# Second attention: the maximum's split in two-input operations, POOL's squaring in one addition and with a larger share

## What is computed

```python
S = jnp.einsum('bhnd,bhmd->bhnm', Q, K) / dh ** 0.5
W_tau = jax.nn.softmax(S, axis=-1)
W_sigma = 1.0 / ((1.0 + jnp.abs(S) / b_) ** 2 + t_ ** 2)
W_sigma = W_sigma / W_sigma.sum(axis=-1, keepdims=True)
tau = jnp.einsum('bhnm,bhmd->bhnd', W_tau, V).transpose(0, 2, 1, 3).reshape(B, N, D)
sigma = jnp.einsum('bhnm,bhmd->bhnd', W_sigma, V).transpose(0, 2, 1, 3).reshape(B, N, D)
f = 0.5 * tau + 0.5 * sigma
```

## Time and profile before

| | |
|---|---|
| time, median of 3 runs | 3559.43 us (3557.44 to 3564.81) |
| profiled execution, span | 3560.9 us |
| DVE busy in it | 2905.9 us, 82% |
| TensorE busy | 2950.8 us, 83% |
| ACT busy | 2449.7 us, 69% |
| POOL busy | 1854.7 us, 52% |
| products on POOL (L1402), 256 | 923.0 us, mean 3606 ns |
| large additions on POOL (L1399), 256 | 453.4 us, mean 1771 ns |
| squares on DVE (L1628), 256 | 222.1 us, mean 867 ns |
| casts on DVE (L1567), 64 | mean 2505 ns |
| narrow additions on POOL (L1397), 256 | 75.9 us, mean 297 ns |

### The profile page before, as it was taken

How to read it: one execution, slowest core, us unless ns; L and a number is a source line. 1 busy time by engine, 2 the same in 40 slices (tenths; PEclk the granted TensorE clock), 3 DMA queues, 4 the chain that set the end, 5 groups by cost and what they waited for, 6 DMA issues and landing times. The chain is left out here.

```text
span 3560.9 us, 64791 instructions
## 1 busy us (share of the span) xinstructions
PE 2950.8 (83%) x19824; PEld 1285.0 (36%) x19824; DVE 2905.9 (82%) x5109; ACT 2449.7 (69%) x3005; POOL 1854.7 (52%) x1283
## 2 busy tenths in 40 slices
PE   4987999999798897478788788878878888885699
PEld 3753444444576454222222222222222222222455
DVE  5996777777499666699999999999999999997665
ACT  3973656656497453288888888888888888885354
POOL 3210000000121444188888888888888888885354
PEclk9987999999799798699999989998999999897699
DMA  3002111110000000200000000000000000000000
GB/s 88 0 0 99 35 33 33 32 33 25 1 1 0 1 1 0 81 14 11 10 13 10 10 11 13 10 10 12 12 10 11 13 10 10 12 5 1 1 13 12
DMA packets 48969, 62.18 MB, mean 17 GB/s; under 512 B 8464, under 2 KB 27920, under 8 KB 48880
## 3 DMA queue, kind: packets, MB, share of 16 engines
q1 hardware_dynamic: 48880, 61.08, 5.5%
HBM read 45.60 MB, written 14.68 MB: 17 GB/s over the span
## 5 line engine op out<-in xcount | busy, mean ns | idle before, releaser
L1402 POOL TENSOR_TENSOR a_sg<-a_sg,a_shifted 128x1600 f32<-128x1600 f32 x256 | 923.0, 3606 | 21.4
L1524 ACT ACTIVATE a_pt<-a_pb 128x1024 f32<-128x1024 f32 x512 | 526.5, 1028 | 310.0 <-PE a_pb L1442 308.8
L1604 DVE TENSOR_REDUCE a_mx<-a_pm 128x1 f32<-128x1024 f32 x512 | 622.5, 1216 | 89.3 <-PE a_pm L1442 81.6
L1612 DVE TENSOR_SCALAR a_sg<-a_pa 128x1024 int32<-128x1024 int32 x512 | 617.3, 1206 | 29.0 <-PE a_pa L1442 28.3
L1287 DVE TENSOR_REDUCE a_mx<-a_pm 128x1 f32<-128x512 f32 (+3 forms) x768 | 404.0, 550 | 158.6 <-PE a_pm L1126 150.4
L1458 PE MATMUL a_po<-a_pt,a_Vh 128*32 128x512 f32 x2048 | 527.8, 639 | 2.2 <-ACT a_sg L1543 2.2
L1458 PE MATMUL a_po<-a_sg,a_Vh 128*32 128x512 f32 x2048 | 527.7, 639 | 0.0
L1214 ACT ACTIVATE a_pt<-a_pb 128x512 f32<-128x512 f32 (+3 forms) x768 | 337.2, 501 | 268.6 <-PE a_pb L1140 96.4
L1539 ACT ACTIVATE a_sg<-a_sg,a_parh 128x2048 f32<-128x2048 f32 x256 | 514.0, 2008 | 0.0
L1543 ACT ACTIVATE a_sg<-a_sg 128x2048 f32<-128x2048 f32 x256 | 492.5, 1924 | 0.0
L1399 POOL TENSOR_SCALAR a_shifted<-a_sg,a_parh 128x1584 f32<-128x1584 f32 x256 | 453.4, 1771 | 0.1
(11 more groups left out here) (244 smaller groups left out, 6061.9 us busy)
## 6 DMA issues: line engine op xcount, KB each, us to landing
all_Q<-q_parts SPq DMA_DIRECT2D x384, 48.0 KB
all_K<-k_parts SPq DMA_DIRECT2D x384, 48.0 KB
q_parts<-p_parts SPq DMA_DIRECT2D x16, 384.0 KB, 2.6
k_parts<-p_parts SPq DMA_DIRECT2D x16, 384.0 KB, 2.6
all_Q<-a_rows SPq DMA_DIRECT2D x128, 6.0 KB
out_dram<-all_X SPq DMA_DIRECT2D x8, 256.0 KB, 2.3
sw_raw<-in_f_We_dram SPq DMA_DIRECT2D x1, 1024.0 KB, 7.1
sw_raw<-in_f_w_gP_dram SPq DMA_DIRECT2D x1, 704.0 KB, 11.0
```

What stands on the lines that cost most here:

```text
L1402: nc.gpsimd.tensor_tensor(buf[:, :, 0:CUT], buf[:, :, 0:CUT], shifted[:], ALU.mult)\
L1524: nc.scalar.activation(pt[(j - LT) % 4][:, i, :], pb[:], ACT.Exp, scale=SC)\
L1604: nc.vector.tensor_reduce(mx[:, (j // PER) % 2, t:t + 1], pm[:], AX.X, ALU.max)\
L1612: nc.vector.tensor_scalar(sg[(j - LS) % 4][:, i, :].bitcast(I32), pa[:].bitcast(I32), SIGN_OFF, None, ALU.bitwise_and).then_inc(abs_done, 1)
```

## The change

For the split, the reduction L1604 now negates what it writes, so mx holds the negated maximum (low). The first part is written as the larger of low and low, a two-input operation that only rounds to bf16. The second part is low minus the first part, rounded; the remainder in fp32 is the same difference, not rounded; the third part is the remainder minus the second part. These are four operations instead of five, each a TENSOR_TENSOR with both inputs in SBUF, and the last, which signals parts_ready, stands behind the second reduction instead of the second sign-clearing.

On POOL the narrow addition is gone: one addition covers all columns below CUT, and CUT rises from 800 to 864 columns, so POOL's addition and product have 1728 elements and DVE's square has 320. The wait for the parameters stands ahead of the wait for the sign-clearings, and that wait is followed by a NOP of its own. The parameters of a head are copied one head earlier. The matmuls are the same.

```diff
--- before.py
+++ after.py
@@ -1313,8 +1313,7 @@
     UNROLL = PER * RING
     LS, LT, LE, LP = 4, 6, 6, 7
     SC = DH ** -0.5
-    EDGE = 8
-    CUT = 25 * T // 32
+    CUT = 27 * T // 32
     with ExitStack() as ctx:
         m = Mem(nc, ctx, tag)
         Q, K = ([stack[:, r, :] for r in range(RING)] for stack in stacks)
@@ -1383,22 +1382,24 @@
                     if (j - LS) % PER == 0:
                         if some(h, 2):
                             pool.wait_ge(pv_done, PER * (h - 1))
-                        nc.gpsimd.tensor_copy(parh[:, ((j - LS) // PER) % RING, :], par[:, h, :])\
-                            .then_inc(par_ready, 1)
+                        if not some(h):
+                            nc.gpsimd.tensor_copy(parh[:, 0, :], par[:, h, :]).then_inc(par_ready, 1)
+                        if not (isinstance(h, int) and h + 1 >= HEADS):
+                            nc.gpsimd.tensor_copy(parh[:, ((j - LS) // PER + 1) % RING, :], par[:, h + 1, :])\
+                                .then_inc(par_ready, 1)
                         nc.gpsimd.tensor_copy(Vh[:, ((j - LS) // PER) % 2, :, 0:DH + 1], V[:, h, :, :])\
                             .then_inc(vh_ready, 1)
                     buf = sg[(j - LS) % 4]
                     if some(s):
                         pool.wait_ge(sq_pool, s)
+                    pool.wait_ge(par_ready, h + 1)
                     pool.wait_ge(abs_done, 2 * s + 2)
-                    pool.wait_ge(par_ready, h + 1)
+                    pool.nop(nofuse=True)
                     b2 = parh[:, ((j - LS) // PER) % RING, 0:1]
 
-                    nc.gpsimd.tensor_tensor(shifted[:, :, 0:EDGE], buf[:, :, 0:EDGE],
-                                            b2.unsqueeze(2).broadcast_to([P, 2, EDGE]), ALU.add).then_inc(shift_done, 1)
-                    nc.gpsimd.tensor_scalar(shifted[:, :, EDGE:CUT], buf[:, :, EDGE:CUT], b2, 1.0, ALU.add, ALU.mult)\
+                    nc.gpsimd.tensor_scalar(shifted[:], buf[:, :, 0:CUT], b2, 1.0, ALU.add, ALU.mult)\
                         .then_inc(shift_done, 1)
-                    pool.wait_ge(shift_done, 2 * s + 2)
+                    pool.wait_ge(shift_done, s + 1)
                     nc.gpsimd.tensor_tensor(buf[:, :, 0:CUT], buf[:, :, 0:CUT], shifted[:], ALU.mult)\
                         .then_inc(sq_pool, 1)
 
@@ -1552,23 +1553,21 @@
 
                     if j % PER or at(it, j, 1) is None:
                         return
-                    h, top = head(it, j, 1), mx[:, ((j - 1) // PER) % 2, :]
+                    h, low = head(it, j, 1), mx[:, ((j - 1) // PER) % 2, :]
                     if n == 0:
                         dve.wait_ge(max_red, TT * h + TT)
                         if some(h):
                             dve.wait_ge(rows_turned, h)
-                        nc.vector.tensor_scalar(neg3[:, 0, :], top, -1.0, None, ALU.mult).then_inc(chain, 1)
-                    else:
-                        dve.wait_ge(chain, 4 * h + n)
+                        nc.vector.tensor_tensor(neg3[:, 0, :], low, low, ALU.max).then_inc(chain, 1)
                     if n == 1:
-                        nc.vector.scalar_tensor_tensor(rem[:], top, -1.0, neg3[:, 0, :], ALU.mult, ALU.subtract)\
-                            .then_inc(chain, 1)
+                        dve.wait_ge(chain, 3 * h + 1)
+                        nc.vector.tensor_tensor(neg3[:, 1, :], low, neg3[:, 0, :], ALU.subtract).then_inc(chain, 1)
                     if n == 2:
-                        nc.vector.tensor_copy(neg3[:, 1, :], rem[:]).then_inc(chain, 1)
+                        nc.vector.tensor_tensor(rem[:], low, neg3[:, 0, :], ALU.subtract).then_inc(chain, 1)
                     if n == 3:
-                        nc.vector.tensor_tensor(rem[:], rem[:], neg3[:, 1, :], ALU.subtract).then_inc(chain, 1)
-                    if n == 4:
-                        nc.vector.tensor_copy(neg3[:, 2, :], rem[:]).then_inc(parts_ready, 1)
+                        dve.wait_ge(chain, 3 * h + 3)
+                        nc.vector.tensor_tensor(neg3[:, 2, :], rem[:], neg3[:, 1, :], ALU.subtract)\
+                            .then_inc(parts_ready, 1)
 
                 def output(it, j, n):
 
@@ -1601,8 +1600,8 @@
                         if sm is not None:
                             t = 2 * (j % PER) + i
                             dve.wait_ge(max_mm, 2 * sm + i + 1)
-                            nc.vector.tensor_reduce(mx[:, (j // PER) % 2, t:t + 1], pm[:], AX.X, ALU.max)\
-                                .then_inc(max_red, 1)
+                            nc.vector.tensor_reduce(mx[:, (j // PER) % 2, t:t + 1], pm[:], AX.X, ALU.max,
+                                                    negate=True).then_inc(max_red, 1)
                         part(it, j, 2 * i + 1)
                         output(it, j, 2 * i)
                         if ss is not None:
```

## The result

The changed kernel takes 3569.52 us (median, 3565.82 to 3571.20) against 3561.15 for the kernel before, run on the same chip: a ratio of 1.0021, 95% interval 1.0014 to 1.0028. It is slower by 0.2%, 8 us; the forecast was slower by 107. The profiled execution has a span of 3565.8 us and a mean granted clock of 0.894 (3560.9 and 0.911 before).

The account below looks back on a forecast made before the run. Bound: a chain through DVE and POOL in the second attention. Per head 10.11 + 5.89 + 2 x 5.93 + 0.92 = 28.78 us, +1.7 on 27.06, times 63 = +107 us: median 3666 us, range 3530 to 3690.

Parts of the forecast that it names:

- (a): POOL's pieces in the second attention: product grows from 3.61 to 3.88 us, large addition from 1.58 to 1.71 us.
- (b): DVE's square, 320 elements instead of 448, takes 0.12 to 0.13 us less: 0.35 after a product, 0.55 alone.
- (c): Slots paced by POOL: late slot 5.93 us for 5.82, slot after the head slot 5.89 for 5.63; +0.48 per head.
- Nearly free: POOL's narrow addition was said to cost almost nothing today, ending about 0.07 us after the square's end.
- (d): Head slot: first split operation held 1.5 us by POOL's addition, second 2.9 by its product; 10.11 us for 8.87, +1.24.
- E: The end of DVE's square L1628, the moment from which the slots of a head are timed.
- slow-clock time: Late slots after TensorE's wait, put to its 1.2 GHz clock: 0.92 us per head, bounds 0 and twice that.
- (e): Parts ready before the last sign-clearing: 1.3 us off TensorE's wait on paper, void in the forecast.
- rival 1: Head slot: first split operation goes before POOL's addition, one hold stays; 26.60 to 27.52 us a head, 3530 to 3588; chance 0.34.
- (f): Waits: POOL's NOP taken at 0.08 us, bounds 0 and 0.23; earlier parameter copies and negated reduction at no cost.
- Rival 2: First slot of each head: POOL's addition gets ahead of DVE's square; +0.9 us a head, 3590 to 3640 us; chance 0.14.
- Rival 3: Split's two-input operations of this size aren't held by POOL; -2.86 us a head, 3380 us; chance 0.10.

Follow-up runs that it names:

- experiment 1: Unneeded TensorE matmuls added in each head slot: ten in the kernel before, ratio 0.9829; six in the changed kernel, 0.9925, both against the kernel before.
- experiment 6: Changed kernel with split operations moved to GpSimd's idle time: 0.9633, then 0.9320 at 800 columns; with TensorE's transposition later 0.9281 (800), 0.9247 (768), 0.9495 (864).
- experiment 2: Kernel before with the split alone, 1.0026, or GpSimd's part alone at 800 columns, 0.9930; changed kernel at 800 columns, 0.9840.
- experiment 3: Changed kernel with an unneeded memset ahead of the first split operation: 64 elements 1.0025, 512 elements 1.0017, 512 with that operation as scalar_tensor_tensor 3570.2 us.
- experiment 5: Three versions of the changed kernel, each with three probe operations behind squares, varying inputs, type, size and operation; the one time given is 3619.5 us.
- e8_third_early: Changed kernel at 800 columns, third split operation right behind the second, output's addition behind the last sign-clearing: 0.9633 of the kernel before.
- experiment 4: Changed kernel at 800 columns, all four split operations directly behind the square, output's addition behind the head slot's square: 1.0507; with six unneeded matmuls 1.0640.
- e10_split_in_addition: Changed kernel at 800 columns, all four split operations directly behind the square, output's addition behind the head slot's square: 1.0507 of the kernel before.
- e18_probe_late: Changed kernel with 512-element memsets ahead of the head slot's first operation and a third-slot 256-column maximum, plus a fourth-slot 64-column maximum: 3619.5 us.
- fastest kernel: Changed kernel at 768 columns, held operations behind the head slot's product, TensorE's transposition behind the next slot's first scores: 0.9247 of the kernel before, 3290.8 us.

## Why the prediction was right or wrong

- *What bounds the stage.* Right, and shown: the chain through both engines (experiment 1: 26.16 and 26.66 against 26.14 and 26.60) with the holds as its largest removable part (experiment 6).
- *(a), (b), (c).* Right: product 3.88, addition 1.71, the idle slot's square 0.57, late slot 5.90 for 5.93, the slot after the head slot 5.81 for 5.89. "Nearly free" for the narrow addition was wrong as a price of removing it (25 us with NOP and copies, experiment 2), but inside the whole change it is already in the chain.
- *(d), the step that failed.* "If it takes its turn at E, the new first operation waits until E + 1.6." The addition did start first, 0.02 us ahead, and the first operation passed, at most 0.18 us in all 64 heads where the forecast had 1.5. The second operation was then not late, and the one hold stayed one, 2.81 us for 2.54. That the first operation isn't held is shown, also at 0.56 us behind the addition's start (experiment 3); why is only read from the cases of experiment 5. Priced at +1.24 in the head slot, it measured +0.08 (8.95 against 8.87). That is 1.16 of the 1.47 us by which a head came out below 28.78 (27.31); the rest is 0.19 of slow-clock time (0.73 for 0.92) and 0.11 in the other slots.
- The Trainium skill's rule in "SBUF — State Buffer", section "Who interferes with whom", that the second to issue blocks, lets the first operation go first if it was issued first, and the trace agrees with that result. The rows show starts and not issues: by its start the operation was second by 0.02 us, so the order of starts isn't the order that counts here. I had let the trace's narrow addition speak against the rule; but that row showed an addition that started 0.04 us after a square's start, not one that found an operation of 8 columns standing behind a square.
- *(e).* The wait before the transposition remained, 1.86 us in the mean of 62 where rival 1 had 1.65; it now ends with the output's addition L1591 right behind the parts, not with the parts. With it the low clock remained, in 61 of 62 heads (58 before) and for longer (stage mean 0.88 for 0.92), and still it cost less: 0.73 us for the 0.92 kept. Rival 1's hope that the clock stays high didn't come true by itself; with 6 added matmuls it gave 3536 where I had 3530.
- *(f).* The idle time between a product and the next GpSimd instruction went from 0.23 to 0.25 us, so the NOP shows as 0.02, not the 0.08 taken. Rival 1 had asked for a NOP of 0.1 or more; its order came without that, so its condition was wrong too. The copies, in GpSimd's idle time, cost nothing that shows. A run without the NOP wasn't tried.
- *Rivals.* Rival 1 is what happened, inside its 3530 to 3588: chain 26.60 forecast, 26.56 measured (8.95 + 5.81 + 2 x 5.90). That rival's time was closer than the forecast's, but the reason it gave for the order, the NOP, was not the cause. Rival 2 didn't occur in the changed kernel (in none of 57 heads) but did in e8_third_early: 2.05 for the square instead of 0.68, and 1.06 us more for the first two slots (37 heads against 9). Its +0.9 was near that, though its own terms, 1.71 - 0.5, give 1.2. Rival 3 fell: the third is held 2.81.
- *Chances.* The forecast with 0.42 stood on a turn order that one pair of rows had to carry. A row that spoke for caution was there: the addition beside a running square starts 0.50 us before the square's end and takes only 0.37 us more than otherwise (1.95 for 1.58), so the start of an instruction isn't yet the moment at which it needs the turn.

## What to carry to other kernels

In this stage a small two-input VectorE operation took 0.16 us by itself and up to 3.55 us, GpSimd's whole product, when it was held: first find where GpSimd stands idle, and put it there, even if GpSimd then has to wait for it (190 us here). Two such operations in a row beside GpSimd are worse than one, because the first hold delivers the second into the next (experiment 4). A granted clock below 1 beside a wait of TensorE may be time on the path: test it with added matmuls before explaining it. They gained 33 and 61 us in two kernels here and cost 49 in a third.

## What the runs showed of the hardware that was not expected

- Starting first isn't having the turn. VectorE operations of 8 columns passed although GpSimd's one-input addition had started 0.02 to 0.56 us before them, and it paid nothing; with 256 columns it paid 0.24 us, and 0.7 behind a memset.
- GpSimd's addition of 864 x 2 columns takes 1.70 us behind GpSimd's own product, but ends 1.49 to 1.58 after the end of a square that it had to wait for: some 0.12 to 0.21 us of it, an estimate from these rows, need no turn.
- Behind a square without a gap, the output's addition of e10_split_in_addition passed when GpSimd's addition started 0.13 us or more after the square's start (17 of 17) and was held when that started at 0.05 (45 of 45). The one first operation of e18_probe_late with 0.20 us of idle time ahead was held too.
- An operation with one of its two inputs in PSUM isn't held. In the fastest kernel L1589, which reads `ptr` in PSUM and `rz` in SBUF, starts 1.21 us into the product and takes 0.28:

```profile
2416.77 0.28 DVE L1589 TENSOR_TENSOR a_fw<-a_ptr,a_rz 128x128 f32<-128x128 f32 x1
...
2415.56 3.47 POOL L1405 TENSOR_TENSOR a_sg<-a_sg,a_shifted 128x1536 f32<-128x1536 f32 x1
```

- For the square, hundredths decide. In e8_third_early it takes 0.67 to 0.70 us when it starts 0.04 ahead of the addition, and 2.05 in 37 of 43 cases when it starts 0.02 to 0.04 behind it.
